# Grouped attention: the probability times value matmuls of a pair of heads in one run instead of four

## What is computed

```python
qn = layernorm(x, ln_q_g, ln_q_b)
q = qn @ Wq * scale
kv = media @ Wkv
k, v = jnp.split(kv, 2, axis=-1)
...
sim = jnp.einsum('bhid,bhjd->bhij', q, k)
sim = jnp.where(media_mask[:, None, None, :], sim, neg_inf)
attn = jax.nn.softmax(sim, axis=-1)
out = jnp.einsum('bhij,bhjd->bhid', attn, v)
...
x = x + jnp.tanh(attn_gate) * (out @ Wo)
```

## Time and profile before

| | us |
|---|---|
| median of 3 runs | 5985.61 |
| lowest, highest | 5980.05, 5986.08 |
| span of the profiled execution | 5983.1 |
| PE busy | 5528.3 |
| DVE busy | 3035.7 |
| ACT busy | 2979.0 |
| POOL busy | 818.6 |

### The profile page before, as it was taken

One profiled execution on the slowest core, in us unless ns is written; L12 is line 12 of the kernel. 1 busy time (PEld: TensorE's weight loads), 2 busy tenths in 40 slices (PEclk: granted clock), 3 DMA queues, 4 the chain that ended last, 5 costly groups with the idle time before them and its releaser, 6 DMA issues. The chain is left out here.

```text
span 5983.1 us, 115762 instructions
## 1 busy us (share of the span) xinstructions
PE 5528.3 (92%) x43160; PEld 4534.1 (76%) x43160; DVE 3035.7 (51%) x5324; ACT 2979.0 (50%) x5599; POOL 818.6 (14%) x1090
## 2 busy tenths in 40 slices
PE   7999999999998798799999969868999999999997
PEld 6888888888886576577777759547888888888886
DVE  3444444444444334577677756343444444444444
ACT  4554554554553455576666730234554454454552
POOL 1111111101101132111011132001101111111101
PEclk9999999999998899899999989988999999999998
DMA  1000000000000000121111100110000000000000
GB/s 50 8 1 8 8 1 8 8 1 8 1 1 15 24 0 0 43 46 33 33 45 33 34 30 0 69 38 26 8 1 8 8 1 8 8 1 8 1 1 28
DMA packets 32466, 98.18 MB, mean 16 GB/s; under 512 B 8320, under 2 KB 19840, under 8 KB 30848
## 3 DMA queue, kind: packets, MB, share of 16 engines
q1 hardware_dynamic: 32000, 91.43, 5.4%
HBM read 58.77 MB, written 2.10 MB: 10 GB/s over the span
## 5 line engine op out<-in xcount | busy, mean ns | idle before, releaser
L975 DVE CUSTOM_DVE_ANT_0 L_attn_probs<-L_attn_ps_s,L_attn_bias 128x1608 f32<-128x1608 f32 x512 | 938.5, 1833 | 942.7 <-PE L_attn_ps_t L838 933.5
L1075 ACT ACTIVATE L_attn_pT<-L_attn_ps_t 128x512 f32<-128x512 f32 (+1 forms) x1536 | 746.2, 486 | 1239.3 <-PE L_attn_ps_t L838 1239.3
L838 PE MATMUL L_attn_ps_t<-ident,L_attn_probs 128*128 128x128 f32 (+1 forms) x6656 | 1009.4, 277 | 18.2 <-DVE L_attn_pT L982 7.2
L838 PEld LDWEIGHTS L_attn_ps_t<-ident,L_attn_probs 128*128 128x128 f32 (+1 forms) x6656 | 752.0, 140 | 217.6 <-issue 136.2
L1098 ACT ACTIVATE L_attn_probs<-L_attn_probs,L_attn_negmax 128x1601 f32<-128x1601 f32 x512 | 832.0, 1625 | 2.6 <-DVE L_attn_negmax L975 2.6
L862 PE MATMUL L_attn_ps_u<-L_attn_pT,L_attn_v_sb 128*64 128x256 f32 (+1 forms) x6656 | 830.5, 387 | 0.0
L862 PEld LDWEIGHTS L_attn_ps_u<-L_attn_pT,L_attn_v_sb 128*64 128x64 f32 (+1 forms) x6656 | 433.1, 136 | 243.9 <-issue 45.5
L821 PE MATMUL L_attn_ps_s<-L_attn_ctx_hi,L_attn_g_hi 128*128 128x402 f32 x2048 | 509.8, 371 | 38.5 <-issue 31.5
L1514 DVE CUSTOM_DVE_ANT_0 L_cross_probs<-L_cross_ps_s,L_cross_bias 128x1608 f32<-128x1608 f32 x256 | 467.1, 1825 | 69.6 <-PE L_cross_ps_s L1363 49.3
L1358 PE MATMUL L_cross_ps_t<-ident,L_cross_probs 128*128 128x128 f32 (+1 forms) x3328 | 480.3, 283 | 22.4 <-DVE L_cross_v_sb L1520 19.4
L821 PE MATMUL L_attn_ps_s<-L_attn_ctx_lo,L_attn_g_hi 128*128 128x402 f32 x2048 | 468.2, 350 | 0.0
(11 more groups left out here) (276 smaller groups left out, 9133.2 us busy)
## 6 DMA issues: line engine op xcount, KB each, us to landing
L_attn_ctx_in<-in_ctxT SPq DMA_DIRECT2D x16, 804.0 KB, 4.5
L_cross_k_mixed<-L_cross_k_hi SPq DMA_DIRECT2D x64, 201.0 KB, 3.5
L_cross_k_mixed<-L_cross_k_lo SPq DMA_DIRECT2D x64, 201.0 KB, 4.3
memory_ctx<-in_ctx SPq DMA_DIRECT2D x8, 832.0 KB, 5.9
L_cross_ctx<-in_ctxT SPq DMA_DIRECT2D x8, 804.0 KB, 5.9
memory_ctxT<-in_ctxT SPq DMA_DIRECT2D x8, 804.0 KB, 4.3
A<-in_L_mlp_w SPq DMA_DIRECT2D x4, 1024.0 KB, 6.0
L_attn_mask_in<-in_mask SPq DMA_DIRECT2D x16, 200.5 KB, 4.4
```

The source lines that it names most:

```text
L838: ins = pe.transpose(ps_t[g % 2][0:w, (k % 4) * P:(k % 4 + 1) * P], source[:, k * P:k * P + w], st.ident[:, :])
L975: dve.tensor_tensor_reduce(out=by_chunk(probs[qt]), in0=by_bank(ps_s), in1=by_chunk(bias), scale=-1.0, scalar=BIG, op0=ALU.add, op1=ALU.mi ...
L1075: act.activation(pT[j % 2][s // 2][0:w, tiles[0]:tiles[-1] + 1, s % 2 * P:(s % 2 + 1) * P], ps_t[g % 2][0:w, 0:P * len(tiles)].rearrange(" ...
```

## The change

In steps 0, 1 and 2 no `pv` runs any more. In step 3 all four parts of the previous pair run one behind the other, after `turn(3)` and before the value part of an odd step. The waits of the parts for the copied transposes stand in front of them as before; where j is odd, the wait of part 0 is for the last value part of the round instead. The wait for `u_ready` (`ps_u` has been read) moves from step 1 to step 3. After the last batch the separate last part of the pair before the last goes away. DVE, ACT, POOL and SP have the same instructions in the same order.

```diff
--- before.py
+++ after.py
@@ -906,16 +906,15 @@
                             make_v(rnd, r, kind)
                         if started or s >= 2:
                             turn(rnd, 3, r, kind)
-                        if s == 0 and finishing:
-
-                            wait_turned(rnd if j % 2 else rnd - 1, 3, TILES * ((j - 1) % 2),
-                                        "first" if first and j == 2 else kind)
-                            pv((j - 2) % NJ, 3)
-                        if s > 0 and started:
-                            if s == 1 and finishing:
+                        if s == 3 and started:
+                            if finishing:
                                 pe.wait_ge(u_ready, J - 1)
-                            wait_turned(rnd, s - 1, TILES * (j % 2), kind)
-                            pv((j - 1) % NJ, s - 1)
+                            for part in range(len(PV_TILES)):
+                                if part == 0 and j % 2:
+                                    fills.wait_taken(pe, taken, rnd, ("V", V_PARTS - 1), kind)
+                                else:
+                                    wait_turned(rnd, part, TILES * (j % 2), kind)
+                                pv((j - 1) % NJ, part)
                         if r % 2 == 1 and r < V_PARTS:
                             make_v(rnd, r, kind)
                         if started or s > 0:
@@ -949,8 +948,6 @@
 
             J, rnd = J_ALL, J_ALL // 2
             turn(rnd, 3, 0, "over")
-            wait_turned(rnd - 1, 3, TILES, "last")
-            pv(NJ - 2, 3)
             pe.wait_ge(exped, TILES * J)
             for g in (0, 1, 2):
                 turn(rnd, g, 0, "over")
```

## The result

The changed kernel takes 6308.76 us (median of 4 runs, 6302.88 to 6315.40) beside 5984.24 us of the kernel before; the ratio is 1.0533, 95% interval 1.0496 to 1.0570. It is 324.5 us slower where 275 were forecast (6261), inside the range of 6204 to 6318.

What follows compares the result with a forecast made beforehand. PE was taken as the bound; emptied steps return only what the DVE and ACT chain leaves: +4.31 - 0.50 - 1.13 - 0.49 = +2.19 us per pair, 275 for two layers on 5985.61, giving 6261 us, range 6204 to 6318.

Steps and rivals of the forecast that it cites:

- What bounds the kernel; transitions: PE is a stream of matmuls without holes; each run of 64-column matmuls carries about 0.25 us of entry and exit.
- Steps 0 to 2 emptied: Emptied steps take the opening's 5.46, 6.90, 5.47 us, set by waits; per pair they give back 0.50, 1.13 and 0.49.
- the even step's chain: Turn 3, DVE's row maxima, ACT's exponential and g_high, DVE's g_low and copy of turn 1, next turn 3: 5.46 us.
- The step with the statistics: Once per batch, 0.7 us more on DVE in the same chain; gains 0.46 us in place of 0.49.
- Step 3: Takes 52 pv instructions in place of 12: +4.31 us per pair, entry and exit paid once, nothing waiting there.
- The loop's jump: PE's 3.00 us idle at the loop's jump back is the jump's own and stays: 0 us change, at best all gone.
- the second rival: The 52-instruction run hides the loop's jump and the slow start behind it: 4.6 us at ten jumps, 6215 us; 7%.
- The range: 6204 to 6318 us, from 0.15 us either way on each gated step, three per pair over 126 pairs.
- The first: PE stays the bound and only transitions count: -0.74 us per pair, 5892 us, faster; 4%.
- The third: Idle gaps of PE drop the clock for one group of scores per pair: +197 us, 6458 us; 5%.
- The fourth: The steady stage has slack the opening lacks, so half of the stalls go: 184 us less, 6077 us; 5%.

Runs made afterwards that it cites:

- before_join: Kernel before with `spread_inverse` moved directly behind the pv run of step 3, making two runs of 64-column matmuls one; 6013.14 us, ratio 1.0047.
- after_unrolled: Changed kernel with its eight batches written out in place of a loop over six of them; 6208.67 us, ratio 1.0364 against the kernel before.
- after_swap: Changed kernel with DVE's `g_low` behind the copy of turn 1 in steps 0 and 2, not ahead of it; 6177.84 us, ratio 1.0316 against the kernel before.
- before_late: Kernel before with step 3 reordered: turn 3, turn 0, value part, pv run, `spread_inverse`, turns 1 and 2; 5958.84 us, ratio 0.9947.

## Why the prediction came out as it did

**What bounds the kernel; transitions.** Right. PE was the bound, and a run does carry about 0.25 us of entry and exit: `before_join` wins 0.27 of stream by one run fewer. At three runs fewer that is about 0.75 us per pair, against 3.1 of new waiting (5.05 taken out of steps 0 to 2 less 1.91 given back). The Trainium skill, page "TensorEngine Tiling (Array Packing)", section "Key Properties", says that a change of the tiling mode drains the TensorE; the 0.27 agrees with that in kind, but no run shows that a drain is what it consists of.

**Steps 0 to 2 emptied.** Right in kind and, outside the loop, to 0.01 us: 5.47, 6.90, 5.46 in `after_unrolled`, from the opening of the trace of before. The releasers are the named ones and one more, ACT's copy of turn 3 ahead of an odd value part (128 waits of 0.36 us), which the opening has too and which is therefore in its 6.90. `after_swap` showed the even step's chain by cutting it. The term failed in size inside the loop: 5.54, 6.96 and 5.53 us. The prediction's sentence that fell short is that the opening "gives the new step lengths by measurement"; it gives those of a written-out batch. 0.2 us per pair in the 96 pairs of the loops is 19 us. The step with the statistics gained 0.39 in place of 0.46 for the same reason (6.58 to 6.19, and 6.12 in `after_unrolled`).

**Step 3.** +4.35 per pair (7.46 to 11.81) in place of +4.31, 5 us in all. The entry is 0.05 longer behind a turn 3 that has waited (554.08 - 553.83 = 0.25 against 0.20). Nothing waits inside the run, as said.

**The loop's jump.** Taken at nothing, with a bound only on the side of gain (the second rival). It went the other way: 22 + 25 became 28 + 46 us, 27 us more. With 19 and 5 this makes 51, and accounts for the 50 us between the 275 forecast and the 324.5 measured (330.5 between the two profiled executions, so a few us stay open).

**The range.** That the time lies inside it is in part luck. Its bounds were set by 0.15 us on each gated step, and the steps used less than half of that; half of the miss came from the jumps, for which it had no room on the side of loss.

**The rivals.** The first (faster, 5892) needed the three steps to give back over 4.31 us; they gave 1.91. The second is refuted at its place: the long run stands ahead of the jump and the idle time is there all the same, longer. The third: the window of 1000 us has a granted clock of 0.99, and in the pair shown above (541.30 to 571.20) it is 1.00: gaps of 0.2 to 0.6 us in three steps of four cost no clock. Behind a jump the first matmuls ran at the lower level, for some time at least, in all ten cases of the changed kernel, but only in eight of the kernel before: after 2.86 and 3.38 us of idle time the twelve scores took 2.32 us at a granted clock of 1.00, after 2.92 and 3.00 us 4.18 and 3.86. The warning in the Trainium skill, page "TensorE: Matmul & The Clock Gate", section "Why this matters for your kernels", of idle gaps between bursts agrees with 18 of these 20 jumps; the short gaps of this change did not set it off. The fourth: no slack, rather 0.07 less than in the opening.

## What to carry to other kernels

Work that keeps the busiest engine occupied between a producer and its consumer is cover, and its place is worth more than its transitions: before gathering runs into one, read for every place that they leave how long the chain through the other engines is there. Stretches of the same trace where the run is missing (the opening, the end) give the new lengths directly, but take them from the same form of code, loop or written out, or compare the links of the chain in both forms: here the one that differs stood in DVE's timeline of the kernel before (0.55 against 0.48 us). Gathering pays where the run that moves stays between the fill of a buffer and its next use, as `before_late` did.

## What the runs showed of the hardware that had not been expected

A step whose chain goes PE, DVE, ACT, DVE, PE is 0.07 us longer inside a hardware loop than in the same code written out (5.53 to 5.55 against 5.47 us), and the row maxima start 0.55 against 0.49 us behind the transpose that releases them. The jump back of PE's loop over 8 pairs of heads cost between 3 and 10 us of PE's time, half or more of it idle time for which the profile names no cause; written out, the kernel before gained 35 us. Among ten jumps of one execution with 2.9 to 3.4 us of idle time each, the granted clock fell behind eight and stayed at 1.00 behind two, and these two were not the shortest (2.86 and 3.38 us).
